# Cross-attention keys computed ahead as transposed units kept in DRAM, with Q's chain on ScalarE and the out projection over four PSUM banks

## The chip, the cores and the metric

The kernel runs on one core of a Trainium2 chip. Times are microseconds (us) on the device. TensorE (PE in the profile) does matmuls and transposes and writes to PSUM, here eight banks of 128 x 512 f32. VectorE (DVE), ScalarE (ACT) and GpSimd (POOL) compute, SyncE (SP) issues most DMAs. Each engine has a queue that it works through in order; semaphores join the queues.

## The reference, cut to what matters

Two layers over x of 4 batches x 512 rows x 512 columns and a context of 4 x 512 x 256. Every step is x = x + f(layernorm(x)).

1. A selective scan on the context, gated by x: `state = state * exp(d_t * A) + (d_t * u_t) * B_t`, `y_t = state . C_t`, 512 channels, 16 states, 512 steps, for each batch; then `y * silu(z)`, z being the normalised x.
2. A feed-forward layer 512 to 2048 to 512 with ternary weights and activations rounded to 8 bits by row.
3. Cross-attention of 16 heads of 128: `q = rmsnorm(x @ Wq) * gq`, `k = rmsnorm(ctx @ Wk) * gk` over each head's 128 columns, `v = ctx @ Wv`, `softmax(q k^T / sqrt(128)) v`, and `@ Wo`.
4. A mixture of 8 experts (two for each row) and a shared one.

Keys and values depend on the context and the weights alone; the queries depend on x.

## The kernel before, in words

The program is one queue by hand for each engine, with loops of the hardware around what repeats (`for_batches`, `for_groups`). It has four stages.

**Prologue.** The scan of batch 0, in eight rounds (`pair`, two rounds to a turn of the loop), each of two states for every channel. On VectorE a round is `times_b` (L951), four `scans` (L959), `times_c` (L970) for each state, and beside them the ternary weights (`ternary`). On ScalarE it is `decay` (L655) and the sums and copies of weights (`w_sums`, `w_out`), on TensorE `y_sum`, which adds a round's 2 x 4 tiles in PSUM (`ps<-xc,ident` and its like, L1334), and then `w_turned`. `times_b` of a round waits for `y_sum` of the one before. SP loads `bc` (the B_t and C_t rows, L408) and the weights for the rounds.

**Turns**, b = 0 to 3. A turn begins with `scan_end` (its gate product is L1021), then `in_quant` and the feed-forward layer in four row tiles (`ffn1`, `ffn2`, and both with the transposes of another tile between, `ffn1_with_turned`, `ffn2_with_turned`). The first three also prepare the scan of batch b + 1 (`scan_a`, `scan_b`, `scan_c`). Then comes the attention of batch b in eight groups of two heads.

**A group.** TensorE makes the rows of Q, K and V (256 columns) into the two banks `pp`. VectorE copies Q and K out (`rows_out`, L1116); ScalarE squares them by head (L786), VectorE adds eps (`mean_square`, L1170), POOL raises to -1/2 (`row_rms`, L554), VectorE scales Q (`q_scale`, L1178). TensorE transposes K and Q, ScalarE copies K^T with its gain and V (L792), VectorE copies Q^T (L1182). Scores go into the two banks `ps`, ScalarE takes exps with the key's norm as scale (L798), TensorE multiplies by V (banks `po`, `pd`), VectorE adds the exps (`key_sums`, L1188, L1192), TensorE sums them to denominators, ScalarE copies these (`denominators_out`, L809), VectorE takes reciprocals (`recip`, L1201). The out projection of group g - 1 runs in group g through the two banks `px`, in four parts `out_proj(k0, h)`, each two row tiles; `add_out` (L1156) scales each by its reciprocal and adds it to x. In the first three turns VectorE runs, between these, the scan of batch b + 1: two states in each group.

In a group g > 0 VectorE's queue before is: rows of Q and K with `times_b` and `add_out` between, `q_scale`, `add_out`, Q^T, both `scans`, both `key_sums`, `times_c(0)`, `add_y(0)` (L977), `recip(0)`, `recip(1)`, `times_c(1)`, `add_y(1)`. Weights come by `w_load` (L413), each into one buffer, issued when the rows that used it are done.

**Experts**, in batches of rows, from about 1895 us on.

`PP_OFF`, `PP_FIRST`, `PP_USES` and `W` in `SEG_SIZE` number the uses of the banks, from which the semaphore counts follow. `mm` (L1334) is the one line of all matmuls; transposes of Q and K have L1555, those of the feed-forward layer L1447 and L1520.

Of the kernel before, what the change touches and what calls it, by code (L numbers as in the profile page):

```python
# [49 lines left out]
SEG_SIZE = {"A": 2, "XQ": 4, "F1": 4, "B": 2, "F2T": 4, "F2": 1, "C": 4, "AP": 4, "W": NT * H, "POST": 4, "TERN": 5 * TC}  # L50
# [24 lines left out]
PP_OFF = {"Q": 0, "K": 2, "V": 4, "KT": 6, "QT": 7, "D": 6 + 2 * GH}  # L75
PP_FIRST = {**PP_OFF, "K": 0, "V": 2, "Q": 3}
PP_STEP = {"KT": 2, "QT": 2}
PP_USES = 6 + 3 * GH
assert PP_USES % 2 == 0


def program(nc, t):
    ctx = ExitStack()
    with ctx:
# [8 lines left out]
        x3_dram = nc.dram_tensor("x3_dram", (B, L, DM), F32).ap()  # L93

# [7 lines left out]
        minus_magic = sb("minus_magic", [P, 1])  # L102
        conv_w = sb("conv_w", [P, EC, DC])
# [50 lines left out]
        qraw, kraw = qk_raw[:, 0], qk_raw[:, 1]  # L154
# [7 lines left out]
        ctx_ssm = dsum  # L162

# [19 lines left out]
        squared = dsum[:].rearrange("p s (i d) -> p (s i) d", d=D)  # L183
        ss = sb("ss", [P, 2, NT * GH])
        ssv = sb("ssv", [P, 2, NT * GH])
        rms = sb("rms", [P, 2, NT * GH])
# [88 lines left out]
        sq_done = sem("sq_done")  # L275
        ssv_done = sem("ssv_done")
# [41 lines left out]
        def pp_at(G, kind, j, first=False):  # L318

            use = (PP_FIRST if first else PP_OFF)[kind] + j * (3 if first and kind == "V" else PP_STEP.get(kind, 1))  # L320
            return use % 2, G * (PP_USES // 2) + use // 2 + 1

        def w_at(turn_, g, k, h):


            halves, off = turn_
            assert off[("W", 0)] % 2 == 0
            return k % 2, halves["px"] + off[("W", 0)] // 2 + g * (NT // 2 * GH) + k // 2 * GH + h + 1
# [21 lines left out]
        dram = t  # L350

# [27 lines left out]
        def _(sp):  # L379
# [16 lines left out]
            def bc_store(s, turn_):  # L396
                if not isinstance(s, int):
                    for i in range(GH):
                        sp.wait_ge(hc_done[i], s * NG + 1)
# [10 lines left out]
            def w_load(which, g):  # L410
                name, dst, s, chunk = {"k": ("Wk", wk, wk_in, CC), "q": ("Wq", wq, wq_in, NC), "v": ("Wv", wv, wv_in, CC)}[which]
                src = dram[name].rearrange("(c p) w -> p c w", p=P)
                sp.dma_start(dst[:], src[:, :, bass.ds(g * GW, GW)]).then_inc(s, 16)  # L413

# [22 lines left out]
            def pair(j, which):  # L437

                for odd in range(2):
                    r = j * 2 + odd  # L440
                    sp.wait_ge(stage_used[odd], j)
                    w_stage(r, odd, which)
                    for i in range(GH):
                        sp.wait_ge(hc_done[i], r)
                        bc_load(bc_first[odd][:, i], (bc_odd_in if odd else bc_in)[i], r * GH + i)
            for j in range(1, HG // 2):
                pair(j, 1)
            with sp.Fori(HG // 2, TC // 2) as j:
                pair(j, 2)
            sp.dma_start(ctx_att[:], dram["ctxT"][0].rearrange("(c p) l -> p c l", p=P)).then_inc(ctx_att_in, 16)  # L450
            for w in "kqv":
                w_load(w, 0)
            wo_load(0)

# [3 lines left out]
            def turn(b, off, scan):  # L458
                turn_ = turn_of(b, off)
                if scan:  # L460
                    bc_store(b + 1, turn_)
# [3 lines left out]
                def group(g, nxt):  # L465

                    for kind, which in (("K", "k"), ("Q", "q"), ("V", "v")) if is_first(g) else (("Q", "q"), ("K", "k"), ("V", "v")):
                        bank, n = pp_at(b * NG + g, kind, 1, is_first(g))
                        sp.wait_ge(pp_full[bank], n)
                        if nxt is not None:  # L470
                            w_load(which, nxt)
                        elif which == "q" and not scan:
                            sp.dma_start(s_w3, dram["s_w3T"].rearrange("(c p) m -> p c m", p=P)).then_inc(sw_in, 16)
                    if not is_first(g):
                        bank, n = w_at(turn_, g - 1, NT - 1, GH - 1)
                        sp.wait_ge(px_full[bank], n)
                        wo_load(g)

# [21 lines left out]
                if scan:  # L500
                    sp.dma_start(ctx_att[:], dram["ctxT"][b + 1].rearrange("(c p) l -> p c l", p=P)).then_inc(ctx_att_in, 16)
                    wo_load(0)
                sp.dma_start(x3_dram[b].rearrange("(t p) d -> p t d", p=P), xc[:]).then_inc(x3_stored, 16)
            for_batches(sp, turn)
# [17 lines left out]
        def _(pool):  # L522
            nc.gpsimd.memset(ones[:], 1.0).then_inc(const_set, 1)
            nc.gpsimd.memset(minus_half[:], -0.5).then_inc(const_set, 1)
            nc.gpsimd.memset(minus_magic[:], -MAGIC).then_inc(const_set, 1)

            def diagonals(s):

                if isinstance(s, int):
# [16 lines left out]
            pool.wait_ge(const_set, 3)  # L546
# [5 lines left out]
            def row_rms(G, j, place):  # L552
                pool.wait_ge(ssv_done, 2 * G + place + 1)
                nc.gpsimd.tensor_tensor(rms[:, j], ssv[:, j], minus_half[:, 0:NT * GH], ALU.pow).then_inc(rms_done, 1)  # L554

            rstd(0, 0)
            def turn(b, off, scan):
# [6 lines left out]
                else:  # L564
# [12 lines left out]
                def group(g):  # L577
                    G = b * NG + g
                    for place, j in enumerate((1, 0) if is_first(g) else (0, 1)):
                        row_rms(G, j, place)  # L580
# [5 lines left out]
            for_batches(pool, turn)  # L586
# [8 lines left out]
        def _(act):  # L595
# [98 lines left out]

            scan_a(0, before_turns)
# [14 lines left out]
            def pair(j, which, last=False):  # L710
                for odd in range(2):
# [1046 lines left out]
```

## Time and profile before

| | us |
|---|---|
| median of 3 runs | 2219.43 (2218.64 to 2219.79) |
| profiled execution | 2218.66 |
| its span | 2216.7 |
| TensorE busy | 1985.3 (90%) |
| VectorE busy | 1661.4 (75%) |
| ScalarE busy | 953.3 (43%) |
| POOL busy | 172.7 (8%) |
| TensorE's mean granted clock | 0.939 of full speed |

The span is what the profile covers; the execution's time has some 2 us around it. Busy times are those of instructions, overlaps within an engine counted once. In rows of the timeline the columns are start, length, engine, line and operation, `out<-in` by the program's names, shape, and the number of instructions drawn together; brackets give the idle time before and what ended it. An f32 matmul leaves more than one record, so `x4` of `px<-wo,oT 128x512` are two matmuls.

### The profile page before, as it was taken

How to read it: one execution, taken by the hardware profiler on the slowest of the kernel's cores; microseconds unless marked ns; L12 is line 12 of the kernel's file. 1: busy time of each engine (PE TensorE's matmuls, PEld its weight loads, DVE VectorE, ACT ScalarE, POOL GpSimd, SP SyncE). 2: the span in 40 equal slices, each digit the busy share in tenths (PEclk: the TensorE clock that was granted, in tenths of full speed). 3: DMA queues.
4: the chain of work that ended last, by engine and by line, in shares of the span. 5: the costliest groups of instructions: out<-in, count | busy, mean ns of one | idle time of the engine just before them, and what ended most of it. 6: DMA issues, size and time to landing. Idle time of an engine off the chain costs nothing.

```text
span 2216.7 us, 25518 instructions
## 1 busy us (share of the span) xinstructions
PE 1985.3 (90%) x7548; PEld 1155.7 (52%) x7548; DVE 1661.4 (75%) x2271; ACT 953.3 (43%) x2208; POOL 172.7 (8%) x120
## 2 busy tenths in 40 slices
PE   6545798999989889999898999996899999899999
PEld 2222345656654556656445565662556666454554
DVE  2999567999995789999867999998553434356555
ACT  3544255455543555555346455552443434221221
POOL 0000001100010110100101010010011101000000
PEclk8777898999999999999998999998999999899999
DMA  3223011212111011222101121221122323100100
GB/s 121 76 76 114 10 40 33 72 57 80 62 57 58 32 54 51 77 62 76 67 20 38 54 79 57 76 66 38 48 58 53 75 51 67 48 32 6 39 19 19
DMA packets 90732, 122.79 MB, mean 55 GB/s; under 512 B 8880, under 2 KB 52528, under 8 KB 90176
## 3 DMA queue, kind: packets, MB, share of 16 engines
q1 hardware_dynamic: 79104, 113.89, 16.1%
q0 software_dynamic: 10768, 6.82, 2.2%
q10 hardware_dynamic: 816, 1.57, 0.2%
q8 instruction: 19, 0.31, 0.1%
q14 instruction: 25, 0.20, 0.0%
HBM read 119.90 MB, written 8.65 MB: 58 GB/s over the span
## 4 chain that ended last, share of the span: by engine, by line
issue 37%; PE 34%; DVE 24%; POOL 2%; DVEq 1%; DMA 1%; ACT 1%; POOLq 0%; SPq 0%; ACTq 0%
PE pp L1334 11%; PE px L1334 11%; DVE arena L959 10%; DVE arena L970 5%; PE ps L1334 5%; DVE arena L951 3%; PE pp L1555 2%; PE po L1334 2%; PE pd L1334 2%; DVE dsum L1192 1%; DVE qk_raw L1116 1%; DVE dsum L1188 1%; POOL bc L535 1%; POOL arena L541 1%; POOL rms L554 1%
## 5 line engine op out<-in xcount | busy, mean ns | idle before, releaser
L959 DVE TENSOR_TENSOR_SCAN arena<-arena 128x512 f32<-128x512 f32 x256 | 290.0, 1201 | 1.8
L1334 PE MATMUL px<-wo,oT 128*128 128x512 f32 x512 | 251.7, 616 | 23.6 <-DVE xc L1156 23.2
L1334 PE MATMUL ps<-qkT 128*128 128x512 f32 x512 | 252.9, 605 | 3.3 <-ACT hbuf L798 3.0
L798 ACT ACTIVATE hbuf<-ps,shift,rms 128x512 f32<-128x512 f32 x256 | 198.6, 777 | 127.4 <-PE ps L1334 119.9
L1334 PE MATMUL pp<-wq,xnT 128*128 128x256 f32 x1024 | 237.1, 391 | 2.9 <-issue 1.5
L786 ACT ACTIVATE dsum<-qk_raw 128x128 f32<-128x128 f32 x512 | 151.2, 296 | 185.4 <-DVE qk_raw L1116 185.4
L1156 DVE SCALAR_TENSOR_TENSOR xc<-px,rden,xc 128x512 f32<-128x512 f32 x256 | 187.6, 748 | 41.6 <-PE px L1334 33.7
L1334 PEld LDWEIGHTS pp<-wq,xnT 128*128 128x128 f32 x1024 | 198.0, 196 | 31.2 <-ACT xnT L773 4.1
L554 POOL TENSOR_TENSOR rms<-ssv,minus_half 128x8 f32<-128x8 f32 x64 | 105.0, 1640 | 960.1 <-DVE ssv L1170 960.1
L655 ACT ACTIVATE arena<-arena,a_neg 128x512 f32<-128x512 f32 x256 | 161.3, 709 | 21.5 <-DVE arena L959 16.6
L1334 PEld LDWEIGHTS ps<-qkT 128*128 128x128 f32 x512 | 90.9, 193 | 127.0 <-issue 76.8
L1334 PEld LDWEIGHTS px<-wo,oT 128*128 128x128 f32 x512 | 96.8, 197 | 105.5 <-issue 61.8
L1116 DVE COPY qk_raw<-pp 128x512 f32<-128x512 f32 x128 | 87.8, 686 | 69.9 <-PE pp L1334 69.7
L1334 PE MATMUL pp<-wk,ctx_att 128*128 128x256 f32 x512 | 121.0, 383 | 16.1 <-DVE qk_raw L1116 16.1
L1334 PE MATMUL po<-hbuf,v_sb 128*128 128x512 f32 x256 | 130.7, 592 | 0.0
L869 ACT ACTIVATE oT<-px 128x512 f32<-128x512 f32 x72 | 43.0, 597 | 201.5 <-PE px L1334 201.5
L951 DVE TENSOR_TENSOR arena<-arena,bc 128x2048 f32<-128x2048 f32 x56 | 127.7, 2280 | 2.3 <-DVE v_sb L921 2.0
L1334 PE MATMUL pd<-hbuf,v_sb 128*128 128x512 f32 x256 | 126.0, 615 | 0.0
L1334 PEld LDWEIGHTS pp<-wk,ctx_att 128*128 128x128 f32 x512 | 95.3, 190 | 49.4 <-issue 28.3
L1334 PE MATMUL pp<-wv,ctx_att 128*128 128x256 f32 x512 | 116.8, 380 | 2.6 <-DVE qk_raw L1116 2.5
L970 DVE TENSOR_TENSOR arena<-arena,bc 128x2048 f32<-128x2048 f32 x52 | 118.0, 2274 | 0.0
L977 DVE TENSOR_TENSOR arena<-arena 128x2048 f32<-128x2048 f32 x48 | 110.0, 2291 | 3.4
(198 smaller groups left out, 2972.4 us busy)
## 6 DMA issues: line engine op xcount, KB each, us to landing
bc<-bc_dram SPq DMA_DIRECT2D x56, 512.0 KB, 5.3
wq<-in_Wq SPq DMA_DIRECT2D x32, 512.0 KB, 4.7
wo<-in_Wo SPq DMA_DIRECT2D x32, 512.0 KB, 3.3
hbuf<-in_w SPq DMA_DIRECT2D x8, 1024.0 KB, 5.2
wk<-in_Wk SPq DMA_DIRECT2D x32, 256.0 KB, 2.5
wv<-in_Wv SPq DMA_DIRECT2D x32, 256.0 KB, 2.5
xs<-in_x SPq DMA_DIRECT2D x4, 1024.0 KB, 5.1
xnT<-bc_dram SPq DMA_DIRECT2D x8, 512.0 KB, 7.3
```

The lines of the kernel that those rows point to most:

```text
L554: nc.gpsimd.tensor_tensor(rms[:, j], ssv[:, j], minus_half[:, 0:NT * GH], ALU.pow).then_inc(rms_done, 1)
L655: nc.scalar.activation(dA[i][:, e], delta[:, e], ACT.Exp, scale=a_neg[:, e, bass.ds(g * GH + i, 1)]).then_inc(exp_done[i], 1)
L786: nc.scalar.activation(squared[:, i], raw[:, k, h * D:(h + 1) * D], ACT.Square, accum_out=ss[:, j, i:i + 1]).then_inc(sq_done, 1)
L798: nc.scalar.activation(pT[:, h, k], ps[s_use % 2][:], ACT.Exp, bias=shift[:, 0:1], scale=rms[:, 1, k * GH + h:k * GH + h + 1]).then_inc(p_ ...
L951: V.tensor_tensor(hb[i], du, bc_i[:, 0:1, :].broadcast_to((P, EC, L)), ALU.mult).then_inc(dbu_done[i], 1)
L959: V.tensor_tensor_scan(hb[i][:, e], dA[i][:, e], hb[i][:, e], 0.0, ALU.mult, ALU.add).then_inc(scan_done[i], 1)
L970: V.tensor_tensor(dst, hb[i], bc_i[:, 1:2, :].broadcast_to((P, EC, L)), ALU.mult).then_inc(hc_done[i], 1)
L977: V.tensor_tensor(u, u, hb[i], ALU.add).then_inc(y_added, 1)
L1116: V.tensor_copy(dst[:, 2 * j:2 * j + 2, :].rearrange("p t w -> p (t w)"), pp[bank][:]).then_inc(pp_drained[bank], 1)
L1156: V.scalar_tensor_tensor(xc[:, k], px[bank][:], rden[:, h, k:k + 1], xc[:, k], ALU.mult, ALU.add).then_inc(px_drained[bank], 1)
L1334: return nc.tensor.matmul(out, lhsT, rhs, start=first, stop=last, **kw)
L1555: m = nc.tensor.transpose(pp[bank][:, k * P:(k + 1) * P], raw[:, k, h * D:(h + 1) * D], ident[:])
```

## The change

- **Units.** K^T of a group of heads and a batch is a unit, 32 in all. `k_unit` (TensorE) multiplies `wk` by the context so that K^T comes out transposed, one bank of `pp` for each head; ScalarE (`k_out`) squares the bank into `k_sq` and copies it with the key gain to a stage; eight one-column matmuls sum the squares, ScalarE copies these with eps; SP (`k_dma`) reloads `wk` when the unit's matmuls are done and stores the stage (512 KB) to `kt_dram`. POOL (`key_rms`) raises the sums of many units at once.
- **Where.** 18 units (groups 0 to 5 of batches 0 to 2) in the prologue's rounds, (3, 2, 2, 2, 2, 2, 2, 3), ahead of `y_sum` on TensorE; two in each of the first three turns, one before `scan_end`, one after `ffn2(3)`; eight in the last turn, at five places of its feed-forward part. `scan_a` of both halves now precedes `scan_end`.
- **A group** loads its K^T (`kt_load`) after the last scores of the group before. V stays, through the banks `ps`. Q's squares, eps, scaling and Q^T copy are all on ScalarE, from PSUM; `rows_out`, `mean_square`, `q_scale` and `qT_out` leave VectorE.
- **Out projection.** `out_proj(2, 0)` goes through the banks `ps`, the other three parts through `px`; denominators go through `px`. Scores wait for `o2_added`.
- **VectorE's order** in a group changes as shown. On SP, POOL, TensorE and ScalarE the loops over rounds, on SP and POOL also that over turns, are written out.

```diff
-PP_OFF = {"Q": 0, "K": 2, "V": 4, "KT": 6, "QT": 7, "D": 6 + 2 * GH}
+PP_OFF = {"Q": 0, "QT": 2}
 # SP
+            def k_dma(n, G, groups, stage, g_next, ctx_next=None):
+                bank, at_ = k_at(n, groups, "KT", 1)
+                sp.wait_ge(pp_full[bank], at_)
+                if g_next is not None:
+                    w_load("k", g_next)
+                if ctx_next is not None:
+                    ctx_load(ctx_next)
+                for h in range(GH):
+                    bank, at_ = k_at(n, groups, "KT", h)
+                    sp.wait_ge(pp_drained[bank], at_ + 1)
+                sp.dma_start(kt_dram[G], stage).then_inc(k_stored[n % 2], 16)
+                    if not (isinstance(g, int) and g == NG - 1):
+                        sp.wait_ge(ps_full[1], (G + 1) * (GH * NT // 2))
+                        kt_load(G + 1)
 # POOL
+            def key_rms(b, end, groups, cols):
...
+                nc.gpsimd.tensor_tensor(dst, src, half, ALU.pow).then_inc(rms_k_done, 1)
 # ACT
+            def k_out(n, G, groups, stage, par, stored):
...
+                    nc.scalar.activation(k_sq[:, h], pp[bank][:], ACT.Square).then_inc(k_squares, 1)
...
+                    nc.scalar.activation(stage[:, h], pp[bank][:], ACT.Copy, scale=kgain[:, 0:1]).then_inc(pp_drained[bank], 1)
...
+                    nc.scalar.activation(ssv_k[:, bass.ds(G * (GH * NT) + h * NT, NT)], pp[bank][:, 0:NT], ACT.Identity, bias=eps[:, 0:1],
+                                         scale=1.0 / D).then_inc(pp_drained[bank], 1)
+            for r in range(TC):
+                j, odd, which = r // 2, r % 2, 1 if r < HG else 2
+                w_sums(j, odd, which)
+                for i, (n, G) in enumerate(round_units(r)):
+                    k_out(n, G, 0, k_stage_first[n % 2], n % 2, n // 2)
+                    if i < GH and r + 1 < TC:
+                        decay(0, r + 1, i)
+                w_out(j, odd, which)
+                    if is_first(g):
+                        xn_out()
+                        act.wait_ge(k_stored[1], stored_after(b) * 16)
+                        squares(0)
+                        squares(1)
+                        mean_squares()
+                        v_rows_out()
                         decays(0)
                     else:
+                        decays(0)
+                        squares(0)
+                        decays(1)
+                        squares(1)
+                        mean_squares()
+                        v_rows_out()
+                    q_out()
+                    for h in range(GH):
+                        qT_out(h)
 # DVE, a group that isn't the first
+                        if scan:
+                            times_b(b + 1, g, 0)
+                        add_out(g - 1, 0, 0)
+                        if scan:
+                            times_b(b + 1, g, 1)
+                            scans(b + 1, g, 0)
+                        add_out(g - 1, 0, 1)
+                        add_out(g - 1, 2, 0)
+                        add_out(g - 1, 2, 1)
                         key_sums(G, 0)
+                        if scan:
+                            scans(b + 1, g, 1)
+                    key_sums(G, 1)
+                    if scan:
+                        times_c(b + 1, g, 0)
+                    recip(0)
+                    recip(1)
...
+                    if scan:
+                        add_y(b + 1, g, 0)
+                        times_c(b + 1, g, 1)
+                        add_y(b + 1, g, 1)
 # PE
+            def k_unit(n, groups, loads):
+                pe.wait_ge(ctx_att_in, loads * 16)
+                pe.wait_ge(wk_in, n * 16 + 16)
+                for h in range(GH):
...
+                    for c in range(CC):
+                        m = mm(pp[bank][:], wk[:, c, h * D:(h + 1) * D], ctx_att[:, c], c == 0, c == CC - 1)
+                    m.then_inc(pp_full[bank], 1)
+                for h in range(GH):
...
+                    pe.wait_ge(k_squares, n * GH + h + 1)
+                    for k in range(NT):
+                        m = mm(pp[bank][:, k:k + 1], k_sq[:, h, k * P:(k + 1) * P], ones[:, 0:1], True, True)
+                    m.then_inc(pp_full[bank], 1)
+            for r in range(TC):
+                for n, G in round_units(r):
+                    k_unit(n, 0, G // NG + 1)
+                for i in range(GH):
+                    y_sum(r, i)
+                w_turned(r // 2, r % 2, 1 if r < HG else 2)
                 if scan:
                     scan_a(b + 1, turn_, 0)
+                    scan_a(b + 1, turn_, 1)
+                    ks(0, 1)
                 scan_end(b, turn_)
...
+                else:
+                    ks(0, 2)
...
+                        if k0 and h == 0:
+                            mm(ps[k % 2][:], oT[:, h, k * P:(k + 1) * P], wo[:, h], True, True).then_inc(o2_full[k % 2], 1)
```

## Rows read from the trace of the kernel before

**Rows 1.** The page, busy time of each engine.
```profile
PE 1985.3 (90%) x7548; PEld 1155.7 (52%) x7548; DVE 1661.4 (75%) x2271; ACT 953.3 (43%) x2208; POOL 172.7 (8%) x120
```
**Rows 2.** Windows: stretch, length; busy PE, PEld, DVE, ACT, POOL; clock, DMA share, GB/s.
```profile
100.00:150.00 50.00, 29.65 (x115) 14.74 (x114) 47.96 (x53) 20.48 (x42) 0.00 (x0) 0.73 0.25 92
...
500.00:550.00 50.00, 48.88 (x189) 32.60 (x188) 48.49 (x56) 27.20 (x76) 3.27 (x2) 1.00 0.28 84
```
**Rows 3.** Timeline of TensorE in turn 0: two groups' Q rows begin.
```profile
538.40 7.15 PE L1334 MATMUL pp<-wq,xnT 128*128 128x256 f32 x32
...
577.42 7.15 PE L1334 MATMUL pp<-wq,xnT 128*128 128x256 f32 x32
```
**Rows 4.** Timeline of TensorE in the last turn, a group to the next one.
```profile
1666.03 7.15 PE L1334 MATMUL pp<-wq,xnT 128*128 128x256 f32 x32
...
1674.74 3.62 PE L1334 MATMUL pp<-wk,ctx_att 128*128 128x256 f32 x16
...
1685.08 1.04 PE L1555 MATMUL pp<-ident,qk_raw 128*128 128x128 f32 x8
...
1688.55 3.88 PE L1334 MATMUL ps<-qkT 128*128 128x512 f32 x8
...
1700.84 0.95 PE L1334 MATMUL pp<-ones,dsum 128*128 128x1 f32 x8
...
1704.26 7.15 PE L1334 MATMUL pp<-wq,xnT 128*128 128x256 f32 x32
```
**Rows 5.** Timeline of VectorE in the scan group that begins at 538.40.
```profile
538.98 2.29 DVE L977 TENSOR_TENSOR arena<-arena 128x2048 f32<-128x2048 f32 x1
...
545.93 0.68 DVE L1116 COPY qk_raw<-pp 128x512 f32<-128x512 f32 x1
...
549.33 1.40 DVE L1156 SCALAR_TENSOR_TENSOR xc<-px,rden,xc 128x512 f32<-128x512 f32 x2
...
556.21 1.65 DVE L1178 TENSOR_SCALAR qk_raw<-qk_raw,rms 128x128 f32<-128x128 f32 x8
...
562.52 9.02 DVE L959 TENSOR_TENSOR_SCAN arena<-arena 128x512 f32<-128x512 f32 x8
```
**Rows 6.** Timeline of ScalarE, then its group of kT copies.
```profile
577.66 0.17 ACT L809 ACTIVATE den<-pp 128x4 f32<-128x4 f32 x1 [0.25 <-PE pp L1334]
...
L792 ACT ACTIVATE qkT<-pp,kgain 128x512 f32<-128x512 f32 x64 | 43.9, 685 | 100.3 <-PE pp L1555 100.3
```
**Rows 7.** Timeline of the prologue: two rounds begin on VectorE, and TensorE's wait.
```profile
88.02 2.27 DVE L951 TENSOR_TENSOR arena<-arena,xnT 128x2048 f32<-128x2048 f32 x1
...
110.51 2.27 DVE L951 TENSOR_TENSOR arena<-arena,bc 128x2048 f32<-128x2048 f32 x1
...
119.62 3.78 PE L1334 MATMUL ps<-xc,ident 128*128 128x512 f32 x4 [9.29 <-DVE xc L970]
```
**Rows 8.** The page's DMA issues: count, KB each, median us to landing.
```profile
bc<-bc_dram SPq DMA_DIRECT2D x56, 512.0 KB, 5.3
...
wk<-in_Wk SPq DMA_DIRECT2D x32, 256.0 KB, 2.5
```
**Rows 9.** Timeline of TensorE: after ffn2(3) of turn 0; in_quant of turn 3.
```profile
336.19 3.83 PE L1520 MATMUL ps<-ident,hbuf 128*128 128x128 f32 x16 [4.12 <-DVE hbuf L1003]
...
1535.87 3.92 PE L1447 MATMUL ps<-ident,hbuf 128*128 128x128 f32 x16 [10.80 <-DVE hbuf L1079]
```
**Rows 10.** Timeline of TensorE, first group of turn 0: a wait, then its scores.
```profile
355.02 2.73 PE L1555 MATMUL pp<-ident,qk_raw 128*128 128x128 f32 x12 [2.77 <-DVE qk_raw L1178]
...
357.54 4.53 PE L1334 MATMUL ps<-qkT 128*128 128x512 f32 x8
```
**Rows 11.** POOL beside VectorE, and POOL's group of 8-column powers.
```profile
230.21 3.61 POOL L535 TENSOR_TENSOR bc<-ident,conv_w 128x2048 f32<-128x2048 f32 x1 [199.06 <-DVE arena L970]
...
230.36 4.54 DVE L920 TENSOR_SCALAR oT<-hbuf,w_inv 128x2048 bf16<-128x2048 f32 x1
...
L554 POOL TENSOR_TENSOR rms<-ssv,minus_half 128x8 f32<-128x8 f32 x64 | 105.0, 1640 | 960.1 <-DVE ssv L1170 960.1
```

More of the change, by code:

```diff
@@ L708, in _ @@
             d_times_u(0)
-            def pair(j, which, last=False):
-                for odd in range(2):
-                    w_sums(j, odd, which)
-                    if not (last and odd):
-                        for i in range(GH):
-                            decay(0, j * 2 + odd + 1, i)
-                    w_out(j, odd, which)
-            with act.Fori(0, HG // 2) as j:
-                pair(j, 1)
-            for j in range(HG // 2, TC // 2):
-                pair(j, 2, last=j == TC // 2 - 1)
+            for r in range(TC):
[6 more added lines that the diff above has]
+                w_out(j, odd, which)
             gate_silu(0, 0)
@@ L761, in turn @@
                 hq_out(2)
+                if not scan:
+                    k_outs(3, 5)
                 if scan:
@@ L764, in turn @@
                 hq_out(3)
+                if not scan:
+                    k_outs(5, 7)
                 if scan:
@@ L843, in group @@
                     exps(1)
+                    if is_first(g) and scan:
+                        d_times_u(b + 1)
                     for h in range(GH):
@@ L1491, in ffn1_with_turned, with ks @@
                     ffn1(k, range(2, 4))
+                count = U_TURN if scan else NG
+                def ks(first, end):
+                    for i in range(first, end):
+                        k_unit(unit_at(b, i)[0], b * NG, b + B)
+                for i in range(2):
+                    pe.wait_ge(o2_added[i], b * NG + 1)
                 if scan:
                     scan_a(b + 1, turn_, 0)
+                    scan_a(b + 1, turn_, 1)
+                    ks(0, 1)
                 scan_end(b, turn_)
                 if scan:
-                    scan_a(b + 1, turn_, 1)
                     scan_conv(b + 1, turn_, 0)
+                else:
+                    ks(0, 2)
                 in_quant()
@@ L1511, in turn @@
                 ffn2_with_turned(1)
+                if not scan:
+                    ks(3, 5)
                 ffn2_with_turned(2)
+                if not scan:
+                    ks(5, 7)
                 ffn2(3, 0, 4)
+                ks(count - 1, count)
                 def xn_turned():
@@ L1609, in group @@
-                    turned("QT", 1, qraw)
+                    q_turned(1)
                     scores(0, 0)
```

485 lines of the change are left out of this document (264 added, 221 removed).

## The prediction, made before the changed kernel was run

> **What bounds the kernel now.** First the page's busy shares: TensorE 90%, VectorE 75%, ScalarE 43% [rows 1]. They average over unlike stages, so the windows come next. In the first scan VectorE is full and TensorE a bit over half busy, at a mean granted clock of 0.73; inside the attention of a turn that scans both are full at clock 1.00 [rows 2]. Then the order of work on TensorE: with the scan a group takes 577.42 - 538.40 = 39.0 us [rows 3]; without it, in the last turn, 1704.26 - 1666.03 = 38.2, of which scores to denominators take 1704.26 - 1688.55 = 15.7 [rows 4]. So in a group TensorE and VectorE bind together, and the prologue is VectorE's alone.
>
> **The change, part by part.** I count in the profiled execution: 2218.66 us, a span of 2216.7 and 2.0 around it, 0.8 under the median 2219.43.
>
> *TensorE in a group.* The K rows go (3.62, of which 0.17 lies over the next group of matmuls) and one set of four transposes of each pair, eight in all, 0.87 [rows 4]: 4.3. The last turn's group becomes 33.9.
>
> *VectorE in a scan group* loses four copies of 0.68, eight scalings of 1.65 together [rows 5], two more copies for the turned Q and two small ones: 5.4. Neither engine alone then asks for more than 33.9. But the new order puts recip(0) and recip(1) right behind times_c(0), and recip(1) needs the second denominator, TensorE's last work of the group: S + 15.7 (S is the start of scores), then ScalarE's copy, 0.25 later and 0.17 long [rows 6]: S + 16.2. Everything VectorE does from there to the next scores is serial: recip 0.2; add_y, times_c, add_y, times_b, times_b at 2.27 to 2.29 [rows 5, 7], 11.4; four of the eight scans, 4.5; add_out(0,0), (0,1), (2,0) and (2,1) at 1.40, of which the scores wait for the first three, 4.2 [rows 5]. Sum 20.3; less 0.06 of overlap of queued instructions at each of eight seams, 19.8. add_out(2,0) counts since out_proj(2,0) now goes through the scores' banks and scores wait for its o2_added. TensorE adds 0.4 for the second turned Q. Next S is 16.2 + 19.8 + 0.4 = 36.4 later, with some 0.3 of lost clock (below) 36.8: 2.2 less than 39.0. Bounds 33.9 and 39.0. Six such periods in each of three turns: 18 x -2.2 = -40.
>
> *Loads in the loop.* bc for times_b(1) is asked for after times_c(1) and has an add_y, a times_b and an add_out to land in, about 6 us, against a median of 5.3 [rows 8]: nothing, 1 a group if it lands at 7. kt_load (512 KB) has from the last scores to the next ones, over 20 us, against wk's reload which it replaces: nothing. Storing and reading 32 units adds 32 MB, some 15 GB/s beside the 84 to 92 that the transfer engines move at a share of 0.28 [rows 2]: nothing.
>
> *ScalarE in a group.* Sixteen squares become eight, the two scaled kT copies eight 128-wide scalings and two copies. A scaling is not in the trace: bounds 0.17 (the 4-wide copy) and 0.69 (the 512-wide one) [rows 6]; I take 0.28, since it has a quarter of the columns. Then they end 0.5 before TensorE reaches the first turned Q. At 0.69 they are 3 late, of which scan groups feel little (TensorE waits 2.5 for VectorE there) and the last turn 2.5 a group.
>
> *First group of a turn.* Decays and an activation-table load now stand between v_rows_out and the scalings: scores +2.9, and TensorE idles some 6 us before them, which halves its clock for a while, +1.5. From there to the next scores VectorE has its 5.4 less and starts the scan before the scores, -6.4. Three turns: -6 (bounds -19 and +13, the one part without the other).
>
> *A unit* is four 512-wide f32 matmuls (two records each), which cost what the K rows did, 3.43, and eight one-column ones, 0.81 [rows 4]. wk has one buffer; its reload is issued when the unit's matmuls end and lands 2.5 later [rows 8], 3.1 to the next matmul. A pair is 3.43 + 3.1 + 3.43 + 1.9 (ScalarE's square and copy, then the sums) = 11.9, three are 18.4.
>
> *Prologue.* A round of VectorE is 110.51 - 88.02 = 22.5, and TensorE idles 9.3 of it [rows 7]. Two units (11.9) stand in front of y_sum (eight matmuls like a unit's four, 6.8) and w_turned (sixteen transposes, 3.5, near the 3.83 of sixteen such [rows 9]): 22.2, just VectorE's round, and times_b of the next round waits for y_sum. Round 0 has three units, so y_sum(0) ends 7.5 after VectorE wants it: +7.5. Rounds 1 to 6 +0.3 each and nearly 2 at each of two ctx_att reloads: +5.5. Round 7's three units stand before the last y_sum, on which the gate product waits: +10. That is 23 at full clock. The clock: TensorE's idle 9.29 us now are followed by four records in 3.78 [rows 7], where such four take half of that at full clock, so it is at 1.2 of 2.4 GHz; and in the attention an idle 2.77 us [rows 10] is soon followed by eight scores in 4.53 instead of 3.88 [rows 4]. On SP each unit's store waits for ScalarE's copies, and the bc loads of round r+2 are queued behind it; they have a round to land in: nothing. Gaps of 3.1 inside every unit pair should do the same to stretches of a round with no slack: +10. Sum +33; bounds 0 (all in the idle time) and 77 (18 units at 4.24 on the path).
>
> *Turn heads.* One unit and the second half of scan_a now precede scan_end. In turn 0 TensorE is the chain there: +6.3. In turns 1 and 2 the attention's end gives 3 back: +4 each; into the last turn -2.2. Sum +12 (bounds 0 and 19). The second unit stands behind ffn2(3), where TensorE waits 4.12 for VectorE [rows 9]: nothing; 5.3 a turn if that cover were gone.
>
> *Last turn.* Two units lie in the 10.80 in which in_quant waited for VectorE [rows 9], +0.9; the third +1; four in two pairs stand between feed-forward matmuls that ran without gaps, 2 x 11.9 = +23.8; the eighth is covered; the clock after their gaps +2; groups 1 to 7: 7 x -4.3 = -30.1; first scores -0.6. Sum -3.
>
> Total: -40 - 6 + 33 + 12 - 3 = -4. Profiled 2214.7, median 0.8 above, about 2216.
>
> *A rule against the change.* POOL's pow grows from 8 columns in 1.64 [rows 11] to 144 at once after the prologue, 16 in each scan turn, 64 in the last: at most 0.2 a column, 29, 3.3 and 13 us. While POOL ran L535's 128x2048 product, L920 on VectorE took 4.54 [rows 11]; beside the pow, VectorE's eight scalings took their 1.65 [rows 5]. I count nothing. The Trainium skill, SBUF — State Buffer, section SBUF: two separate sides, says that the port pair which VectorE and GpSimd share is held for a whole instruction and the loser fully blocks. The first row agrees, the second does not. By the rule VectorE would stand still through each pow, the rival "lock" below.
>
> **The rivals.**
> *The loop does not bind* (0.17). If VectorE's queue hides the denominator wait, 33.9 and the 0.3 of clock hold in scan groups too: 18 x (34.2 - 36.8) = -47 more, 2169. For: neither engine has more than 33.9 of work. Against: nothing behind recip(1) can pass it.
> *Units hidden in the prologue* (0.13): w_turned and units fill the 9.3 idle, and the three extra ones replace idle time at the start: 33 better, 2183. Against: y_sum stands behind them in TensorE's order.
> *Prologue serial, the slower side* (0.15). Place: TensorE from the first unit of a round to y_sum's end. At half clock for a whole round, y_sum and two units cost 6.8 + 2 x 3.43 = 13.7 more; low half of the time, 8 x 6.9 = +55: 2271. It decides for slower from 1 us a round beyond my +33 on. For: 0.73 as mean clock there. Against: the longest gap falls from 9.3 to 3.1.
> *Scalings late* (0.08): each at 0.69 and bc landing at 7: last turn +17, scan groups +18: 2251.
> *Lock* (0.07): 3.3 in each scan turn, up to 13 in the last, where V and normalised rows wait; the 144 columns partly behind the gate: +11 to +23, 2233.
>
> **How the numbers follow.** The balance forecast has 0.40; its own range is 2204 to 2228: the steady period within 0.5 (9) and the prologue within 8. A difference under 0.2% (4.4 us) can't be told from none here. Of the forecast, faster 0.18, same 0.15, slower 0.07; both hidden cases are faster (0.30), the last three slower (0.30). Faster 0.48, same 0.15, slower 0.37. Range 2170 to 2252: it reaches to the free loop and the late scalings and leaves out half of the serial prologue.
>
> **What would show it.** The steady scan group on TensorE's Q rows at 36.8 (33.9 or 39 is wrong); VectorE idle about 1.8 a group before the reciprocals, released by ScalarE's den; TensorE idle before px, released by VectorE's xc; last-turn groups 33.9; the gate product (L1021) some 33 later than before; TensorE's granted clock in the prologue near or above 0.73. I am wrong if a prologue round is past 25 us, if ScalarE's scalings release the turned Q, or if VectorE stands still beside the long pow.

## The result, and the profile after

The changed kernel takes 2247.98 us (2246.40 to 2250.56, 4 runs), the kernel before 2219.61 beside it: a ratio of 1.0129, interval 1.0111 to 1.0146. I had forecast 2216, 4 faster; it is 28 slower. It lies inside the range of 2170 to 2252, but the direction is wrong; slower had 0.37. The profiled execution has a span of 2247.7, 31.0 over the span of before, 2216.7.

The page after, busy times and TensorE's clock in 40 slices:

```profile
PE 2045.7 (91%) x7548; PEld 1155.7 (51%) x7548; DVE 1476.5 (66%) x1759; ACT 1023.8 (46%) x2176; POOL 167.1 (7%) x94
...
PEclk8899888899999989999998999998999999899999
```

VectorE lost 185 us of work against [rows 1], and the time rose: so its busy share was not what to look at. TensorE's busy time rose by 60 though it has fewer columns to stream (the keys' transposes are gone), which points to a lower clock under part of its work.

The two windows of [rows 2] after:

```profile
100.00:150.00 50.00, 43.98 (x191) 24.66 (x189) 42.72 (x44) 30.97 (x66) 0.00 (x0) 0.90 0.49 150
500.00:550.00 50.00, 47.66 (x165) 28.23 (x164) 41.99 (x42) 25.41 (x59) 1.64 (x1) 0.97 0.23 74
```

In the prologue the granted clock rose from 0.73 to 0.90, in the attention it fell from 1.00 to 0.97. Where the time went, by the starts of the gate product (VectorE) and of the Q rows (TensorE) in both traces, beside what I had forecast:

| stretch | forecast | measured |
|---|---|---|
| to the gate product of batch 0 | +33 | +44.5 (244.83 to 289.30) |
| gate product to first Q rows, turns 0, 1, 2 | +14.3 | +6.2, +2.8, +1.4 = +10.4 |
| first and second group, turns 0, 1, 2 | -6 | +1.7, +3.7, +1.2 = +6.5 |
| groups 2 to 7 and the way to the next gate product | -40 | -10.3, -8.6, -10.3 = -29.2 |
| last turn, gate product to Q rows | +25.5 | +28.7 |
| last turn, its eight groups | -30.7 | -29.2 |
| experts | 0 | -0.6 |
| sum | -4 | +31.0 |

Each row is rounded by itself; the sum is that of the spans. Three rows make the error: the prologue (11.5), the first two groups (12.5) and the steady ones (10.8).

**Prologue.** VectorE's second times_b of rounds 1, 2, 3 and 6 (before, those of rounds 1 and 2 began at 88.02 and 110.51 [rows 7]), and the gate product:

```profile
99.47 2.29 DVE L1118 TENSOR_TENSOR arena<-arena,xnT 128x2048 f32<-128x2048 f32 x1 [10.49 <-PE pd L1459]
...
125.05 2.29 DVE L1118 TENSOR_TENSOR arena<-arena,bc 128x2048 f32<-128x2048 f32 x1 [2.96 <-PE pd L1459]
...
151.53 2.29 DVE L1118 TENSOR_TENSOR arena<-arena,xnT 128x2048 f32<-128x2048 f32 x1 [4.39 <-PE pd L1459]
...
225.92 2.29 DVE L1118 TENSOR_TENSOR arena<-arena,bc 128x2048 f32<-128x2048 f32 x1 [5.11 <-PE pd L1459]
...
289.30 1.29 DVE L1188 TENSOR_TENSOR arena<-ps,arena 128x512 f32<-128x512 f32 x2 [24.49 <-ACT arena L782]
```

Each waits for y_sum (`pd`); before, none did. From one to the next the rounds take 23.7 to 26.8 us, three of the six more than the 25 that I had named as a sign of being wrong. TensorE in round 1: a unit's sums, the next unit, its sums, y_sum's first matmuls:

```profile
106.68 2.12 PE L1459 MATMUL pp<-ones,dsum 128*128 128x1 f32 x16 [0.70 <-ACT wq L827]
108.66 5.38 PE L1459 MATMUL pp<-ctx_att,wk 128*128 128x512 f32 x8
113.87 0.95 PE L1459 MATMUL pp<-ones,dsum 128*128 128x1 f32 x8
115.30 1.20 PE L1459 MATMUL pp<-ones,dsum 128*128 128x1 f32 x8 [0.48 <-ACT wo L827]
116.36 3.50 PE L1459 MATMUL ps<-xc,ident 128*128 128x512 f32 x4
```

The unit takes 5.38 where full clock gives 3.6, y_sum's four records 3.50 where it gives 1.9. What stands before each is not a long idle time (0.70 and 0.48) but a stretch of one-column matmuls. I had put the low clock down to gaps of 3.1 us, and to 1.2 us a round; it is over 3 in this one. In all eight rounds the second unit takes 5.1 to 5.8 (two of them behind a wait for a context load as well), while the third unit of rounds 0 and 7 takes 3.67 behind just such sums, and y_sum's first records are slow in three rounds: the low clock doesn't follow each time.

**Groups.** Three group starts, and VectorE and TensorE in the group between the first two:

```profile
473.67 3.70 PE L1459 MATMUL pp<-wq,xnT 128*128 128x256 f32 x16
...
510.17 3.70 PE L1459 MATMUL pp<-wq,xnT 128*128 128x256 f32 x16
...
548.36 3.70 PE L1459 MATMUL pp<-wq,xnT 128*128 128x256 f32 x16
```

```profile
474.11 0.18 DVE L1348 RECIPROCAL rden<-den 128x4 f32<-128x4 f32 x1 [1.61 <-ACT den L981]
474.28 2.29 DVE L1144 TENSOR_TENSOR arena<-arena 128x2048 f32<-128x2048 f32 x1
...
486.83 4.57 DVE L1126 TENSOR_TENSOR_SCAN arena<-arena 128x512 f32<-128x512 f32 x4
491.31 1.39 DVE L1322 SCALAR_TENSOR_TENSOR xc<-px,rden,xc 128x512 f32<-128x512 f32 x2
```

```profile
492.09 1.98 PE L1459 MATMUL px<-wo,oT 128*128 128x512 f32 x4 [2.23 <-DVE xc L1322]
...
528.59 3.34 PE L1459 MATMUL px<-wo,oT 128*128 128x512 f32 x4 [2.22 <-DVE xc L1322]
```

The queue arithmetic held to 0.1 us: 510.17 - 473.67 = 36.50, VectorE idle 1.61 before recip(1), TensorE idle 2.23 before px, released by VectorE's xc, all as foretold. But the next group takes 38.19: the same wait of 2.2 is followed there by matmuls at half clock (3.34 for what took 1.98). Of turn 0's five, two take 36.50 and three 38.1 to 38.2. I had allowed 0.3 on the average for that; it is 1.0.

**The first group's tail** (turn 0): the gate's normalisation now stands behind recip(1):

```profile
431.27 0.18 DVE L1348 RECIPROCAL rden<-den 128x4 f32<-128x4 f32 x1 [2.16 <-ACT den L981]
431.37 2.47 DVE L1147 BATCH_NORM_STATS2 ln_st<-xs 128x6 f32<-128x512 f32 x4
...
435.94 2.29 DVE L1144 TENSOR_TENSOR arena<-arena 128x2048 f32<-128x2048 f32 x1 [0.19 <-DVE ln_nm L1159]
```

Before, it lay between the two reciprocals, mostly in time that VectorE waited anyway. Now its 435.94 - 431.37 = 4.6 stand on the serial stretch, behind a wait of 2.16; between the reciprocals 2.2 of them would lie in that wait. The diff shows the move; my sum had no term for it.

**Last turn.** 34.0 a group, forecast 33.9; its head rose by 28.7:

```profile
1859.02 3.70 PE L1459 MATMUL pp<-wq,xnT 128*128 128x256 f32 x16
...
1893.03 3.70 PE L1459 MATMUL pp<-wq,xnT 128*128 128x256 f32 x16
```

### The profile page after: what moved, and what is told of

Read it like the earlier page. It is cut to its first block, busy times and chain, and to the rows that moved or that the text cites. A ratio compares the mean times of both kernels' runs of the same rounds, so it can differ in the third digit from the quotient of the medians.

```text
span 2247.7 us, 25273 instructions
## 1 busy us (share of the span) xinstructions
PE 2045.7 (91%) x7548; PEld 1155.7 (51%) x7548; DVE 1476.5 (66%) x1759; ACT 1023.8 (46%) x2176; POOL 167.1 (7%) x94
## 4 chain that ended last, share of the span: by engine, by line
PE 58%; DVE 17%; issue 16%; ACT 5%; DVEq 1%; DMA 1%; POOL 1%; ACTq 0%; SPq 0%; POOLq 0%
PE ps L1459 17%; PE px L1459 15%; PE pp L1459 10%; PE po L1459 6%; PE pd L1459 6%; DVE arena L1118 4%; DVE arena L1126 3%; DVE arena L1144 3%; DVE arena L1137 2%; PE ps L1604 1%; DVE xc L1322 1%; ACT hbuf L970 1%; PE pp L1726 1%; ACT dsum L822 1%; PE ps L1678 1%
## 5 line engine op out<-in xcount | busy, mean ns | idle before, releaser
L1459 PE MATMUL px<-wo,oT 128*128 128x512 f32 x384 | 210.3, 676 | 73.5 <-DVE xc L1322 73.3
L970 ACT ACTIVATE hbuf<-ps,shift,rms_k 128x512 f32<-128x512 f32 x256 | 198.8, 778 | 125.7 <-PE ps L1459 118.6
L1459 PEld LDWEIGHTS pp<-wq,xnT 128*128 128x128 f32 x1024 | 196.8, 195 | 43.9 <-issue 17.7
L1322 DVE SCALAR_TENSOR_TENSOR xc<-px,rden,xc 128x512 f32<-128x512 f32 x192 | 138.1, 745 | 91.5 <-PE px L1459 89.4
L1459 PE MATMUL pp<-ctx_att,wk 128*128 128x512 f32 x256 | 133.1, 669 | 9.0 <-DMA ctx_att<-in_ctxT 6.2
L942 ACT ACTIVATE qk_raw<-pp 128x128 f32<-128x128 f32 x256 | 67.4, 278 | 127.6 <-PE pp L1459 127.6
L656 POOL TENSOR_TENSOR rms<-ssv,minus_half 128x8 f32<-128x8 f32 x32 | 56.9, 1777 | 900.6 <-ACT ssv L947 900.6
L1332 DVE TENSOR_TENSOR dsum<-hbuf 128x512 f32<-128x512 f32 x64 | 43.7, 683 | 116.2 <-ACT hbuf L970 116.2
L1459 PE MATMUL ps<-wv,ctx_att 128*128 128x256 f32 x512 | 115.7, 379 | 0.0
L1336 DVE TENSOR_TENSOR dsum<-dsum,hbuf 128x512 f32<-128x512 f32 x128 | 88.6, 692 | 40.6 <-ACT hbuf L970 35.9
L964 ACT ACTIVATE qkT<-pp 128x512 f32<-128x512 f32 x64 | 38.2, 597 | 166.6 <-PE pp L1726 166.6
## 6 DMA issues: line engine op xcount, KB each, us to landing
hbuf<-in_w SPq DMA_DIRECT2D x8, 1024.0 KB, 11.5
```

The lines of the kernel that those rows point to most:

```text
L656: nc.gpsimd.tensor_tensor(rms[:], ssv[:], minus_half[:, 0:NT * GH], ALU.pow).then_inc(rms_done, 1)
L942: nc.scalar.activation(qraw[:, k, h * D:(h + 1) * D], pp[bank][:, i * GW + h * D:i * GW + (h + 1) * D], ACT.Square, accum_out=ss[:, h * NT ...
L970: nc.scalar.activation(pT[:, h, k], ps[s_use % 2][:], ACT.Exp, bias=shift[:, 0:1], scale=rms_k[:, bass.ds(G * (GH * NT) + (h * NT + k), 1) ...
L1322: V.scalar_tensor_tensor(xc[:, k], px[bank][:], rden[:, h, k:k + 1], xc[:, k], ALU.mult, ALU.add).then_inc(px_drained[bank], 1)
L1332: V.tensor_tensor(dsum[:, h], pT[:, h, 0], pT[:, h, 1], ALU.add).then_inc(ds_step[h], 1)
L1336: V.tensor_tensor(dsum[:, h], dsum[:, h], pT[:, h, k], ALU.add).then_inc(ds_step[h], 1)
```

## The experiments

My theory had become: (a) order: on TensorE units stand ahead of y_sum, and on VectorE what stands between recip(1) and the scores sets a group; (b) the clock: one-column matmuls in the units, waits for VectorE in the groups, lower it. Its rivals: the units simply cost TensorE their time; the banks hold the groups; VectorE has no room for another order. Ratios are to the kernel before, run on the same chip, with 95% intervals.

**1. Units behind y_sum** (prologue only; in round 0 one stays ahead). TensorE's part of the edit:

```diff
+                for i in range(GH):
+                    y_sum(r, i)
+                w_turned(r // 2, r % 2, 1 if r < HG else 2)
                 for n, G in round_units(r):
                     k_unit(n, 0, G // NG + 1)
-                for i in range(GH):
-                    y_sum(r, i)
-                w_turned(r // 2, r % 2, 1 if r < HG else 2)
```

> The changed kernel with the prologue's units moved behind y_sum and w_turned on TensorE (one of round 0's three stays ahead), the decays ahead of the units' copies on ScalarE, and the bc loads ahead of the unit's stores on SP. Theory (order: y_sum stands behind the units and VectorE waits for it, 31 us over the rounds): the gate product comes near 258 instead of 289.3 and the kernel takes 2217. Rival (the units cost TensorE their time and clock wherever they stand in a round): gate product above 280, 2240 or more.

Measured 2249.77, ratio 1.0147 (1.0130 to 1.0164): nothing gained. The gate product:

```profile
288.22 1.29 DVE L1201 TENSOR_TENSOR arena<-ps,arena 128x512 f32<-128x512 f32 x2 [37.88 <-ACT arena L787]
```

The order helps the rounds, and the kernel gains nothing by it. Round 0 gained 10.7 us (the second times_b at 88.74, not 99.47), and the last y_sum began at 252.22, not 273.00. But the rounds after it took 22.5 to 26.7, four of the six 23.9 or more (before the change 21.2 to 22.5), with units at the low clock in them; the last three units stood ahead of the gate's silu on ScalarE, a fault of my edit (37.88 of waiting); and the first Q rows of turn 0 came at 391.39, as in the change (391.46). The rival was nearer.

**2. Unit sums 128 columns wide** (same values, in every column; ScalarE then copies the first column of each 128)

```diff
-                        m = mm(pp[bank][:, k:k + 1], k_sq[:, h, k * P:(k + 1) * P], ones[:, 0:1], True, True)
+                        m = mm(pp[bank][:, k * P:(k + 1) * P], k_sq[:, h, k * P:(k + 1) * P], ones[:], True, True)
```

> The changed kernel with the eight one-column sums of a unit made 128 columns wide (the same sum in every column), so that TensorE's array is busy in their place. Theory (the stretches of one-column matmuls between a unit's matmuls let the clock fall, and second units and y_sum then run at 1.2 GHz for 1.7 us each): some 3 us a round less, 8 x -3 and a little in the last turn, 2222 to 2230. Rival (only the waits for wk and for ScalarE let it fall): 2246 to 2252.

Measured 2216.82 (10 runs), ratio 0.9999 (0.9989 to 1.0008): 31 us back (29 by the ratios), more than expected, with one widened operand. Its window of 100 to 150, the unit that took 5.38, the second times_b of rounds 1 and 2 and the gate product:

```profile
100.00:150.00 50.00, 44.99 (x216) 25.53 (x215) 46.50 (x48) 34.10 (x76) 0.00 (x0) 1.00 0.55 170
```

```profile
105.11 2.23 PE L1459 MATMUL pp<-ones,dsum 128*128 128x128 f32 x16 [0.70 <-ACT wq L827]
107.17 3.60 PE L1459 MATMUL pp<-ctx_att,wk 128*128 128x512 f32 x8
```

```profile
97.90 2.29 DVE L1118 TENSOR_TENSOR arena<-arena,xnT 128x2048 f32<-128x2048 f32 x1 [8.85 <-PE pd L1459]
...
120.44 2.27 DVE L1118 TENSOR_TENSOR arena<-arena,bc 128x2048 f32<-128x2048 f32 x1
...
272.29 1.29 DVE L1188 TENSOR_TENSOR arena<-ps,arena 128x512 f32<-128x512 f32 x2 [21.37 <-ACT arena L782]
```

Nearly the same idle times (0.70 in both; 0.42 for 0.48), the same matmuls, and the clock stays at 2.4 GHz; the wide sums cost 0.1 us more. So the one-column stretches lowered it. The gate product stands 17.0 sooner: that is the clock's part of the prologue's 44.5, and 27.5 is left, where I had 23 at full clock.

The two spans are 34.4 apart. Beside the prologue's 17.0, the first two groups of the three turns are 11.7 shorter, the last turn's way to its Q rows 7.2 and the other three 2.0 together; the steady groups are 3.5 longer. So a large part of what the first two groups had lost came back, with gate_norm where the change has it: the Q matmuls of a turn's first group (`x32`) take 7.2, not 9.2 to 9.4, and from the first group's scores to the second's it is 43.8 to 43.9, not 45.5 to 45.7, since the wait for add_out(0,1) is now followed by full clock. A unit's sums end 8 us ahead of those Q matmuls; how they act on what comes so much later is not shown.

**3. gate_norm between the reciprocals**

```diff
                     recip(0)
-                    recip(1)
                     if is_first(g):
                         if scan:
                             gate_norm(b + 1, 3 * b + 3)
                         else:
                             moe_norm(0, 0, 0)
+                    recip(1)
```

> The changed kernel with the normalisation of the next batch (gate_norm, 4.6 us on VectorE) back between the first and the second reciprocal of a turn's first group. Theory (it was moved onto the serial stretch behind the second reciprocal): the second group's scores come 4.6 us sooner and TensorE loses less clock, 3 x -4.6 to -6, 2248 to 2232. Rival (something else, the banks, holds the first groups): above 2244.

Measured 2244.27, ratio 1.0119 (1.0095 to 1.0144): 4 less than the change, intervals overlapping, and the value at the rival's bound; the kernel's time doesn't decide. By the trace the first two groups of turns 1 and 2 are 3.5 shorter each, those of turn 0 only 1.2. But 2.2 of those 3.5 lie ahead of the first scores, which the edit doesn't reach: from Q rows to first scores it is 20.7 or 18.5, whatever the edit (runs 4, 5 and 7 have both). From the first group's scores to the second's it is 43.6 in every turn, not 45.5 to 45.7: 2.0, since VectorE's add_y begins 2.8 behind the second group's Q rows, not 5.1. Then TensorE comes sooner to its wait for add_out(0,1), waits longer, and goes on at half clock:

```profile
450.08 3.78 PE L1459 MATMUL px<-wo,oT 128*128 128x512 f32 x4 [3.84 <-DVE xc L1322]
```

The term is real but partly masked: the wait behind it, then the clock, take some of it back. Where that wait is gone it shows more: the scores of the first and the second group of turn 0 in run 4 (gate_norm behind recip(1)), then in run 9 (between the reciprocals, and wide sums):

```profile
413.52 5.88 PE L1460 MATMUL ps<-qkT 128*128 128x512 f32 x8
...
454.92 3.98 PE L1460 MATMUL ps<-qkT 128*128 128x512 f32 x8
```

```profile
390.61 5.88 PE L1460 MATMUL ps<-qkT 128*128 128x512 f32 x8
...
427.96 3.98 PE L1460 MATMUL ps<-qkT 128*128 128x512 f32 x8
```

41.4 and 37.4, in every turn: 4.0.

**4. Scans behind the add_outs**

```diff
                         if scan:
                             times_b(b + 1, g, 1)
-                            scans(b + 1, g, 0)
                         add_out(g - 1, 0, 1)
                         add_out(g - 1, 2, 0)
                         add_out(g - 1, 2, 1)
+                        if scan:
+                            scans(b + 1, g, 0)
```

> The changed kernel with the first four scans of a group moved from ahead of add_out(0,1) to behind add_out(2,1) on VectorE. Theory (VectorE's queue between the second reciprocal and the scores sets the group): add_out(0,1) meets its matmuls, the period falls from a mean of 37.5 to between 34.0 and 34.8, 18 x -3 and some more in the second groups, 2185 (2178 to 2200). Rival (VectorE has no room, the scans then delay the sums of exps and the denominators): period 36 or more, 2225 or more.

Measured 2171.33, ratio 0.9784 (0.9765 to 0.9804): 77 us less than the change, 46 less than before, and below the theory's own numbers. Two group starts, the matmuls that had waited for add_out(0,1), now without a wait, and VectorE's add_out(0,1):

```profile
572.78 3.70 PE L1460 MATMUL pp<-wq,xnT 128*128 128x256 f32 x16
...
606.79 3.70 PE L1460 MATMUL pp<-wq,xnT 128*128 128x256 f32 x16
```

```profile
588.81 1.88 PE L1460 MATMUL px<-wo,oT 128*128 128x512 f32 x4
```

```profile
586.00 1.61 DVE L1322 SCALAR_TENSOR_TENSOR xc<-px,rden,xc 128x512 f32<-128x512 f32 x2
...
591.47 4.56 DVE L1126 TENSOR_TENSOR_SCAN arena<-arena 128x512 f32<-128x512 f32 x4
```

34.01 a group, as in the last turn: TensorE alone. The room for the scans was there, behind the scores.

**5. add_y(0) ahead of the reciprocals**, the scans left where the change has them

```diff
                         times_c(b + 1, g, 0)
+                        add_y(b + 1, g, 0)
                     recip(0)
...
                     if scan:
-                        add_y(b + 1, g, 0)
                         times_c(b + 1, g, 1)
```

> The changed kernel with add_y(0), 2.3 us, ahead of the two reciprocals on VectorE, where it ran before; the scans stay ahead of add_out(0,1). Theory (what stands between the second reciprocal and the scores sets the group, whatever it is): VectorE reaches the second reciprocal at S + 16.9 instead of waiting for S + 16.2, and the chain behind it is 2.3 shorter: period 35.0 at full clock, 18 x -1.6 and up to 18 x -1 of clock, 2200 to 2219. Rival (the place of the scans ahead of add_out(0,1) alone holds TensorE's bank): 2240 or more.

Measured 2188.22, ratio 0.9859 (0.9843 to 0.9876). The theory's side, and below its numbers: the steady group is 34.8 (35.0 expected), and every one is, since TensorE's wait for px is now

```profile
559.97 1.98 PE L1459 MATMUL px<-wo,oT 128*128 128x512 f32 x4 [0.53 <-DVE xc L1322]
```

0.53 and no low clock follows. 2.3 us of VectorE moved off the serial stretch are worth 2.7 a group. So it was the stretch's length, not the scans' place as such.

**6. Denominators 128 columns wide** (in each group of the change)

```diff
-                            m = mm(px[bank][:, k:k + 1], dsum[:, h, k * P:(k + 1) * P], ones[:, 0:1], True, True)
+                            m = mm(px[bank][:, k * P:(k + 1) * P], dsum[:, h, k * P:(k + 1) * P], ones[:], True, True)
```

> The changed kernel with the denominators' one-column matmuls of each group made 128 columns wide. In the changed kernel three of five steady groups take 38.2 us and two 36.5, with matmuls at the low clock behind a wait of 2.2 us. Theory (the wait lets the clock fall, not the denominators, which stand 20 us ahead of it): the mix stays, 2246 to 2250. Rival (the denominators do, as the sums of a unit did): all groups 36.5, 2230 or less.

Measured 2245.93, ratio 1.0114 (1.0096 to 1.0133): as the theory has it. Groups of 36.6 and of 38.1 to 38.3 stand in the same mix. In the groups it is the wait behind which the clock is low, and runs 4 and 5, which take the wait away, have no long groups.

**7. Wide sums and the units behind y_sum**, with the gate's silu ahead of the last copies

```diff
                 w_out(j, odd, which)
+                if r == TC - 1:
+                    gate_silu(0, 0)
```

> The kernel with 128-column sums, and the prologue's units behind y_sum and w_turned as in the run that moved them, now with the gate's silu ahead of the last round's copies on ScalarE. Theory (a round with units cost 24.5 us of TensorE at the low clock, so that the order could not help; at full clock it is under VectorE's 22.5, and then the order does): rounds at VectorE's pace, gate product near 247 instead of 272, turn 0's first matmuls near 258 instead of 275, 2200. Rival (TensorE's sum of work binds the prologue at full clock too): 2213 or more.

Measured 2226.60, ratio 1.0036 (1.0024 to 1.0049): the expectation fails, 10 us worse than wide sums alone (8 by the ratios). The rounds do run nearly at VectorE's pace, and the gate product comes at 253.68 (247 expected). Then turn 0's first matmuls:

```profile
276.93 9.41 PE L1473 MATMUL ps<-dsum,ipT 128*128 128x512 f32 x16 [6.77 <-DMA dsum<-in_ctxT]
```

Three units stand ahead of them, and the load of the scan's context into the squares' buffer, which waits for the last unit's copies, is no longer hidden. All 18 units are in the prologue either way; what comes free in its rounds is needed again at its end.

**8. All four edits** (of 2, 3, 4 and 7)

> All that helped: 128-column sums, the prologue's order, gate_norm between the reciprocals, the scans behind the add_outs. Theory (they act in different stages and add up): 2248 - 77 - 31 - 17 - 6 = 2117, between 2110 and 2130. Rival (what the prologue gains is lost in turn 0 again, TensorE being the bound of both): 2135 or more.

Measured 2141.48, ratio 0.9657 (0.9641 to 0.9673), on the rival's side of my numbers: groups and sums add up, the prologue's order takes away.

**9. The same without the prologue's order** (edits of 2, 3 and 4)

> 128-column sums, gate_norm between the reciprocals and the scans behind the add_outs, with the prologue in the order of the changed kernel. The run with the prologue's order too took 2141.5; moving the units behind y_sum had brought the gate product to 254 but left turn 0's first matmuls at 277, behind three units and a context load that waits for them, and cost 10 us. Theory (that order only moves the wait): without it 2248 - 77 - 31 - 4 = 2136, or 2141.5 - 10 = 2131: 2128 to 2138. Rival (the order helps once the rest is mended): 2145 or more.

Measured 2135.04, ratio 0.9619 (0.9603 to 0.9635), as expected: 113 under the change and 85 under the kernel before. Its window in the attention:

```profile
500.00:550.00 50.00, 49.88 (x178) 30.30 (x177) 47.83 (x46) 28.21 (x67) 1.64 (x1) 1.00 0.25 77
```

**10. Out projection back to two banks**, on top of 9. TensorE's part of the edit:

```diff
-                        if k0 and h == 0:
-                            mm(ps[k % 2][:], oT[:, h, k * P:(k + 1) * P], wo[:, h], True, True).then_inc(o2_full[k % 2], 1)
-                        else:
-                            bank, n = w_at(turn_, g, k, h)
-                            pe.wait_ge(px_drained[bank], n - 1)
-                            mm(px[bank][:], oT[:, h, k * P:(k + 1) * P], wo[:, h], True, True).then_inc(px_full[bank], 1)
+                        bank, n = w_at(turn_, g, k, h)
+                        pe.wait_ge(px_drained[bank], n - 1)
+                        mm(px[bank][:], oT[:, h, k * P:(k + 1) * P], wo[:, h], True, True).then_inc(px_full[bank], 1)
```

> The best kernel so far (2135) with the change's bank part undone: out_proj(2,0) goes through the two px banks like the other three parts, and scores don't wait for it. Theory (in the new order out_proj(0,1), (2,0) and (2,1) follow each other closely, so that with two banks each waits for an add_out of 0.75 and the way there and back): some 1.2 us twice in each of 28 groups, and low clock behind it now and then, 2135 + 67 = 2200 (2185 to 2215). Rival (VectorE and the queue behind hide it, four banks are worth nothing): 2140 or less.

Measured 2156.43, ratio 0.9714 (0.9696 to 0.9731). Two group starts:

```profile
518.49 3.70 PE L1450 MATMUL pp<-wq,xnT 128*128 128x256 f32 x16
...
552.76 3.70 PE L1450 MATMUL pp<-wq,xnT 128*128 128x256 f32 x16
```

34.27 a group, 0.26 more and not 2.4: both sides missed. By the two traces (24.7 apart) the groups make 12.7 of it, the ways from gate product to Q rows 8.5, and the prologue, which the edit doesn't touch, 3.3. The four banks are worth 1% here.

## Why the prediction was wrong, step by step

- **A unit at 3.43 and 0.81, TensorE's group at 33.9, scalings at 0.28, the period by the queues at 36.4.** Right: 3.6 and 0.95 as the rows show them, 34.0, eight scalings in 2.15, 36.50 at full clock.
- **Prologue, "at full clock 23".** The mechanism right (units ahead of y_sum), mis-sized by 4.5: 27.5 with wide sums, some of it still clock (behind the second context load a unit took 5.40). Round 0's third unit cost 8.9 (I had 7.5), the second context load 4.9 (I had under 2).
- **"Gaps of 3.1 inside every unit pair ... +10".** Wrong in its cause and size: 17 us, from the one-column sums, as run 2 shows. Their 0.81 was in the sum as time, and what they do to the matmuls behind them was not. I looked for idle time before low clock, since [rows 7, 10] show it so, and never asked what a stretch that is busy with almost no columns does.
- **First groups, -6.** Wrong: +6.5. For later first scores and the clock behind them I had +4.4 a turn; to the first scores +3.9, +6.1 and +3.6 were measured, so that was right in the sum. The step that failed is "from there to the next scores ... -6.4": -2.4, -2.6 and -2.5 were measured, 3.9 less a turn and 11.7 of the 12.5. The serial stretch was right for steady groups, but in the first one the diff also moves gate_norm behind recip(1), worth 2.0 by run 3 alone and 4.0 where the wait for add_out(0,1) is gone (runs 4 and 9). Clock behind that wait is worth another 1.6 to 1.9 (run 2). That these two add up to the 3.9 was not tried in one run. I had counted what leaves VectorE and not what moved onto its serial stretch.
- **Steady groups, -40.** -29.2. 36.5 was right; the low clock behind the wait for px costs 1.7 in three of five groups (1.0 on the average) and not 0.3. The same wait of 2.2 us has both outcomes, and I had priced the milder one.
- **Turn heads, last turn.** +10.4 for 14.3, and -0.5 for -5.2 in all: sizes of some us, as bounded.
- **The rivals.** "Serial prologue" was the one that came nearest, at a fifth of the price that I had given it. "Scalings late" fell. "Lock" fell: POOL's long pow took 23.31 us, and a gate product beside it its usual 0.68. One operand of that lies in PSUM, and VectorE did nothing else beside the long pow; the stronger rows, with both inputs in SBUF beside the short pow, stand at the end. POOL, then VectorE:

```profile
273.58 23.31 POOL L665 TENSOR_TENSOR rms_k<-ssv_k,minus_half 128x144 f32<-128x144 f32 x1 [242.61 <-ACT ssv_k L833]
...
291.10 0.68 DVE L1188 TENSOR_TENSOR arena<-pd,arena 128x512 f32<-128x512 f32 x1
```

"The loop does not bind" was true of the work and false of the order: run 4 reached its 34.0 by moving one call.

What stays open: why the same wait of 2.2 us has both outcomes, which no run tells; which of the Q chain's parts on ScalarE pays for itself, which was not tried alone; and how the wide sums act on the first groups. The 8.9 us of round 0's third unit were read from one trace.

## What to carry to other kernels

When work leaves an engine, write its new queue out from the last thing it must wait for to the first thing that others wait for, in every variant of the loop body (the first iteration too): that stretch sets the time, not the busy share. A matmul stage that is added between others costs its own time and what it does to the clock of the next ones, so give a sum over partitions a full tile's columns where these are cheap. Before undoing a change, try moving its calls: here one call moved was worth 77 us, one widened operand 29 to 31.

## What the runs showed of the hardware

- TensorE's clock fell to 1.2 GHz behind matmuls of one column (0.95, 0.48 idle and 1.05 us), though not behind every such stretch, and stayed at 2.4 behind the same ones with 128 columns (1.05, 0.38 idle, 1.16): 17 us in the prologue, 29 to 31 in the kernel. A one-column f32 matmul costs nearly what a 128-column one does (0.95 against 1.05 for eight records).
- In the changed kernel a wait of 2.2 us is followed by low clock in three groups of five and not in the others; one of 0.53 (run 5) never was. In the kernel before, 2.77 was once [rows 10], and 2.23 was not, eight records there taking 1.99 as at full clock:

```profile
814.00 1.99 PE L1334 MATMUL pp<-wk,ctx_att 128*128 128x256 f32 x8 [2.23 <-DVE qk_raw L1116]
```

- A small operation on VectorE, 0.16 us elsewhere, took 4.46 beside POOL's 128x2048 product of 4.50, and L920 took 4.54 beside another [rows 11], 1.29 elsewhere. Beside POOL's 16-column pow four operations of L1170 took their usual 1.92 and a 128x2048 product on VectorE its usual 2.29, of which 0.97 lay beside the pow. POOL's rows, then VectorE's:

```profile
381.43 4.50 POOL L643 TENSOR_TENSOR arena<-arena 128x2048 f32<-128x2048 f32 x1
385.89 2.90 POOL L665 TENSOR_TENSOR rms_k<-ssv_k,minus_half 128x16 f32<-128x16 f32 x1
```

```profile
381.50 4.46 DVE L1159 SCALAR_TENSOR_TENSOR ln_nm<-ln_mv,ln_r 128x4 f32<-128x4 f32 x1 [1.12 <-POOL ln_r L652]
385.99 1.92 DVE L1170 TENSOR_SCALAR hbuf<-xc,ln_r,ln_nm 128x512 f32<-128x512 f32 x4
387.82 2.29 DVE L1102 TENSOR_TENSOR arena<-arena 128x2048 f32<-128x2048 f32 x1
```

The Trainium skill, SBUF — State Buffer, section SBUF: two separate sides, has the loser of the shared port pair block for a whole instruction. For POOL's tile products these rows agree with it, for its pow they don't.
